# Three images of a channel norm moved into the state-space scan, and the scan's B products written in place

## What is computed

```python
x_dbl = einsum('bkdl,kcd->bkcl', xs, x_proj_weight)         # xs: 4 directions of the image
dts, Bs, Cs = split(x_dbl, [R, R + N], axis=2)              # R = 6, N = 16 states
delta = softplus(einsum('bkrl,kdr->bkdl', dts, dt_projs_weight) + dt_projs_bias)
h = exp(d_t[..., None] * A) * h + (d_t * u_t)[..., None] * B_t[:, :, None, :]   # per position
y = einsum('bkdn,bkn->bkd', h, C_t)
...                                                          # the 4 directions are added up
mean = jnp.mean(y, axis=1, keepdims=True)
var = jnp.var(y, axis=1, keepdims=True)
return (y - mean) / jnp.sqrt(var + LN_EPS) * ln_g + ln_b
```

## Time and profile before

| | us |
|---|---|
| median of 3 runs | 5211.8 (5211.26 to 5217.86) |
| the profiled execution's own time | 5209.67 |
| its span in the trace | 5207.9 |
| first scan of the selective scan starts | 2719.7 |
| last result of the scan taken | about 5125.5 |
| norm, from its first weight load to the end | 5126.1 to 5207.9 |

### The profile page before, as it was taken

One profiled execution on the slowest core, in us unless ns is written; L12 is line 12 of the kernel. 1 busy time (PEld: TensorE's weight loads), 2 busy tenths in 40 slices (PEclk: granted clock), 3 DMA queues, 4 the chain that ended last, 5 costly groups with the idle time before them and its releaser, 6 DMA issues. The chain is left out here.

```text
span 5207.9 us, 68598 instructions
## 1 busy us (share of the span) xinstructions
PE 4496.8 (86%) x15210; PEld 2101.0 (40%) x15210; DVE 4241.3 (81%) x3460; ACT 3168.8 (61%) x6678; POOL 4079.0 (78%) x1926
## 2 busy tenths in 40 slices
PE   7998797966899999994688888889898888989897
PEld 2333463632566666663452323223222332322222
DVE  4776545554189999999549999999999999999995
ACT  5885555532011111110469888888888888888886
POOL 2544555534088898989659999999999999999993
PEclk9998998988899999997789999999999999999998
DMA  2000101137777787873318788878787778888873
GB/s 55 1 1 10 51 30 44 41 105 229 150 140 149 141 149 143 150 136 60 104 44 200 199 203 201 197 201 201 202 201 191 199 200 202 202 200 202 201 202 94
DMA packets 389221, 733.15 MB, mean 141 GB/s; under 512 B 78332, under 2 KB 119464, under 8 KB 375912
## 3 DMA queue, kind: packets, MB, share of 16 engines
q1 hardware_dynamic: 388968, 730.30, 59.2%
HBM read 594.31 MB, written 82.32 MB: 130 GB/s over the span
## 5 line engine op out<-in xcount | busy, mean ns | idle before, releaser
L2221 POOL TENSOR_TENSOR l_hc<-l_h,l_c_rep 128x1024 f32<-128x1024 f32 x768 | 1797.7, 2370 | 17.9 <-DVE l_h L2292 15.6
L1400 POOL TENSOR_TENSOR l2b_prod<-l2b_v,l2b_attn 128x1568 f32<-128x1568 f32 x276 | 937.4, 3444 | 232.5 <-ACT l2b_attn L1361 117.5
L2292 DVE TENSOR_TENSOR_SCAN l_h<-l_p,l_h,l_bu 128x1024 f32<-128x1024 f32 x448 | 1027.2, 2331 | 4.8 <-ACT l_bu L2129 3.5
L1976 PE MATMUL l_p<-l_stacked,l_pick 96*128 96x512 f32 x1536 | 559.9, 446 | 220.4 <-DVE l_h L2292 203.1
L1448 DVE TENSOR_REDUCE l2b_osum<-l2b_prod 128x32 f32<-128x1568 f32 x384 | 665.7, 1780 | 63.0 <-POOL l2b_prod L1400 59.3
L2210 POOL TENSOR_TENSOR l_pool_bu<-l_du_rep,l_b_sb 128x1024 f32<-128x1024 f32 x256 | 607.6, 2373 | 37.7 <-DMA l_du_rep<-du_scratch 37.5
L2276 DVE TENSOR_TENSOR l_bu<-l_du_rep,l_p 128x1024 f32<-128x1024 f32 x512 | 612.9, 1197 | 21.5 <-DMA l_du_rep<-du_scratch 16.0
L1353 ACT ACTIVATE l2b_logits<-l2b_conv,l2b_this_b 98x512 f32<-98x512 f32 x96 | 66.1, 689 | 860.9 <-PE l2b_conv L1318 860.9
L1976 PEld LDWEIGHTS l_p<-l_stacked,l_pick 96*128 96x128 f32 x1536 | 242.3, 189 | 800.4 <-DVE l_h L2292 643.2
L1985 PE MATMUL l_p<-l_hc,l_y_pick 128*32 128x512 f32 x3072 | 523.4, 606 | 5.9 <-POOL l_hc L2221 5.6
L2292 DVE TENSOR_TENSOR_SCAN l_h<-l_p,l_h,l_pool_bu 128x1024 f32<-128x1024 f32 x224 | 524.2, 2340 | 3.8 <-ACT l_pool_bu L2129 2.8
(11 more groups left out here) (269 smaller groups left out, 8933.6 us busy)
## 6 DMA issues: line engine op xcount, KB each, us to landing
l_du_rep<-du_scratch SPq DMA_DIRECT2D x1536, 256.0 KB, 4.8
l2b_img_high<-qkv_scratch SPq DMA_DIRECT2D x192, 306.2 KB, 5.6
l2b_img_low<-qkv_scratch SPq DMA_DIRECT2D x192, 306.2 KB, 9.4
l_stacked<-l_parts SPq DMA_DIRECT2D x512, 96.0 KB, 3.2
l2b_v<-v_scratch SPq DMA_DIRECT2D x192, 152.0 KB, 6.6
qkv_scratch<-l2a_strip SPq DMA_DIRECT2D x32, 840.0 KB, 5.2
du_scratch<-l_du SPq DMA_DIRECT2D x128, 192.0 KB, 2.1
l_w_raw<-L_w_sed SPq DMA_DIRECT2D x32, 576.0 KB, 3.7
```

Of the source, the lines that this page charges most:

```text
L1400: return eng.tensor_tensor(dst.rearrange("q x (dy dx) -> q x dy dx", dx=WIN), window, attn_half[:, :, unit % 2].rearrange("q x (dy dx) -> ...
L1976: pe.matmul(p_da[p % 2][:, e, :], pick[:, GRP[i] % (Q // DL), :], stacked[:, par, GRP[i] * DL // Q, :], start=True, stop=True).then_inc(s_ ...
L2221: pool.tensor_tensor(hc[:, slot:slot + 2, :], h[:, 2 * p:2 * p + 2, :], c_rep[:, par, :].unsqueeze(1).to_broadcast([128, 2, N]), ALU.mult) ...
L2292: dve.tensor_tensor_scan(flat(h[:, 2 * p:2 * p + 2, :]), flat(p_da[p % 2]), flat(of), state, ALU.mult, ALU.add).then_inc(s_h, 1)
```

## The change

Nothing of what is computed changes. Four things move:

1. **Norm of an image in the next one's scan.** In images 1 to 3, each of the two passes of each direction's loop (c = 2, 3 and c = 4, 5) also handles one norm tile of the image before: 8 tiles an image, 24 in all, each spread over an even and an odd step. The last image's 8 tiles stay in `channel_norm_out`.
2. **Its instructions.** Even step: PE `norm_mm` (the product with `center`) ahead of `replicate(n, k, 0, par)`, into the PSUM bank of B that is free then; ACT `norm_early` (Square and Copy) between `decays 0` and `log_1e`. Odd step: PE `norm_mm` (the product with `mean_w`) at the same place; ACT Ln ahead of `log_1e` and Exp (`norm_rstd`) behind it; DVE the product `xc * rstd`, both in SBUF, between `scan 2` and `times_b 4`; ACT `norm_result` (the affine, into `X`) between `b_copy` and `decays 4`. The next `b_mm` waits for ACT to have read the bank.
3. **B products in place.** `du_rep` becomes six fixed slots of a pair; DVE and POOL write their products back into the slot and the scan reads them there. `bu` and `pool_bu` are gone, and with them the waits for a free buffer. A slot's next transfer now waits for the slot's scan instead of for a product of the ring.
4. **Loops.** Image 0 is written out ahead of the loop, the loop covers images 1 and 2, image 3 stands behind it. SP's loop body becomes a whole direction and also stores two finished tiles of `X` per direction (192 KB each). The three norm weights are loaded at the start of `selective_scan`.

```diff
+            def norm_mm(n, tile, par):
+                pe.wait_ge(s_bu, NB * n + BU0)
+                pe.wait_ge(s_bcp, n)
+                bank = p_b[1 - par][0:C]
+                if par == 0:
+                    pe.matmul(bank, center[:], X[:, bass.ds(tile * N, N)], start=True, stop=True).then_inc(s_xc, 1)
+                else:
+                    pe.wait_ge(s_xsq, tile + 1)
+                    pe.matmul(bank, mean_w[:], rstd[:], start=True, stop=True).then_inc(s_var, 1)
...
+                if tile is not None:
+                    norm_mm(n, tile, par)
                 pe.wait_ge(s_stack[par], stack_count(b, k, c, par))
                 replicate(n, k, 0, par)
...
+            def norm_early(tile, par):
+                bank = p_b[1 - par][0:C]
+                if par == 0:
+                    act.activation(rstd[:], bank, ACT.Square)
+                    act.activation(xc[:], bank, ACT.Copy).then_inc(s_xsq, 1)
+                else:
+                    act.activation(rstd[:], bank, ACT.Ln, bias=eps[:, 0:1], scale=WIDE_VAR_SCALE).then_inc(s_lnv, 1)
...
                 decays(n, k, c, 0)
+                if tile is not None:
+                    norm_early(tile, par)
                 if n1:
                     log_1e(n + 1)
+                if tile is not None and par:
+                    norm_rstd(tile)
                 decays(n, k, c, 1)
...
+                if tile is not None and par:
+                    norm_result(tile)
                 decays(n, k, c, 4)
...
                 scan(n, k, c, 2, par)
+                if tile is not None and par:
+                    dve.wait_ge(s_rstd, tile + 1)
+                    dve.tensor_tensor(xc[:], xc[:], rstd[:], ALU.mult).then_inc(s_xhat, 1)
                 times_b(n, 4, par)
...
-                dve.tensor_tensor(bu[:, at % 2], du_rep[:, slot:slot + 2, :],
+                dve.tensor_tensor(du_rep[:, p], du_rep[:, p],
                                   p_b[par].unsqueeze(1).to_broadcast([128, 2, N]), ALU.mult).then_inc(s_bu, 1)
...
-                user, step_of = (i - RING) % G // 2, (i - RING) // G
-                if user in POOL_PAIRS:
-                    sp_.wait_ge(s_pbu, NP * (n + step_of) + POOL_PAIRS.index(user) + 1 + PBU0)
-                else:
-                    sp_.wait_ge(s_bu, NB * (n + step_of) + DVE_PAIRS.index(user) + 1 + BU0)
+                if not (isinstance(n, int) and n == 0):
+                    sp_.wait_ge(s_h, PAIRS * (n - 1) + p + 1 + H0)
```

More of the change, by code:

```diff
@@ L1705, in local_attention_layout, with selective_scan @@
     }
-def selective_scan(nc, w, X, du_d):
+def selective_scan(nc, w, X, du_d, norm, out):
     K, S, R, DL = 4, 16, 6, 8
@@ L1807, in all_steps, with at, image @@
         def all_steps(step):
-            def at(b, k, c, par, last, eng=None):
+            def at(b, k, c, par, last, tile=None):
                 first = isinstance(b, int) and b == 0 and k == 0 and isinstance(c, int) and c == 0
                 step(b, b * STEPS + (k * CHUNKS) + c, k, c, par, ahead(b, k, c, 1, last), ahead(b, k, c, 2, last),
-                     None if first else ahead(b, k, c, -1, last))
-            def image(eng, b, last):
+                     None if first else ahead(b, k, c, -1, last), tile)
+            def image(eng, b, last, normed):
                 for k in range(K):
@@ L1914, in _ @@
[L1914 to L1923 removed]
+                if not (isinstance(n, int) and n == 0):
+                    sp_.wait_ge(s_h, PAIRS * (n - 1) + p + 1 + H0)
+                    sp_.nop(nofuse=True)
@@ new lines, in replicate_du, with prepare @@
+                for e in range(2):
+                    i = 2 * p + e
+                    src = du_d[par, GRP[i] * DL:(GRP[i] + 1) * DL]
+                    src = bass.AP(src.tensor, src.offset, [[0, S], [N, DL], [1, N]])
+                    sp_.dma_start(du_rep[:, p, e], src).then_inc(s_dur[p], 16)
+            def prepare(m, par):
+                store_du(m, par)
+                for p in range(SPLIT):
+                    replicate_du(m, par, p)
+                if not (isinstance(m, int) and m == 0):
+                    sp_.wait_ge(s_rep, G * (m - 1))
+                    sp_.nop(nofuse=True)
+                restack(m, par)
+                for p in range(SPLIT, PAIRS):
+                    replicate_du(m, par, p)
@@ new lines, in step, with store_tile, direction @@
+            def step(n, par, more):
+                if more:
+                    prepare(n + 1, 1 - par)
+            prepare(0, 0)
+            def store_tile(b, j):
+                tile = b * PER_IMAGE + j
+                sp_.wait_ge(s_res, tile + 1 + RES0)
+                sp_.nop(nofuse=True)
+                sp_.dma_start(out[bass.ds(b, 1), :, bass.ds(j * N, N)].rearrange("b c t -> (b c) t"),
+                              X[:, bass.ds(tile * N, N)]).then_inc(s_out, 16)
+            def direction(first, k, b, pairs):
+                for q in range(pairs):
+                    step(first + 2 * q, 1, True)
+                    step(first + 2 * q + 1, 0, True)
+                    if b is not None and q >= 2:
+                        store_tile(b - 1, 2 * k + (q - 2))
@@ L2001, in y_whole, with step @@
                 mm.then_inc(s_ysum, 1)
-            def step(b, n, k, c, par, n1, n2, before):
+            def step(b, n, k, c, par, n1, n2, before, tile):
                 if k == 0 and isinstance(c, int) and c == CHUNKS - 2:
@@ L2023, in step @@
                 if n1:
-                    b_mm(n + 1, 1 - par, *n1)
+                    b_mm(n + 1, 1 - par, *n1, tile)
                 replicate(n, k, 4, par)
@@ L2202, in times_b @@
                     pool.nop(nofuse=True)
[L2203 to L2210 removed]
+                pool.wait_ge(s_dur[p], replicated(n))
+                pool.nop(nofuse=True)
+                pool.tensor_tensor(du_rep[:, p], du_rep[:, p], b_sb[:, par, :].unsqueeze(1).to_broadcast([128, 2, N]),
                                    ALU.mult).then_inc(s_pbu, 1)
@@ L2315, in _, with channel_norm_out @@
             dve.wait_ge(s_y, B * STEPS + Y0)
-def channel_norm_out(nc, w, X, out):
+def channel_norm_out(nc, X, norm, out):
     DEPTH = 4
@@ L2494, in build @@
         attention_out(nc, w["L2"], X, o_d, x_d)
-        selective_scan(nc, w["L3"], X, du_d)
-        channel_norm_out(nc, w["L3"], X, out)
+        norm = {n: ctx.enter_context(nc.sbuf_tensor("l3n_" + n, shape, F32))
+                for n, shape in (("center", [C, C]), ("mean_w", [C, C]), ("cols", [C, 2]), ("eps", [C, 2]))}
+        selective_scan(nc, w["L3"], X, du_d, norm, out)
+        channel_norm_out(nc, X, norm, out)
 def kernel(**inputs):
```

166 lines of the change are left out of this document (76 added, 90 removed).

## The result

The changed kernel takes 5222.26 us (5217.04 to 5229.19), the kernel before, in the same rounds, 5213.58 (5207.86 to 5220.25): a ratio of 1.0015 with a 95% interval of 1.0009 to 1.0021. The prediction was 5212, with 5202 to 5222 as the forecast's own range and 5178 to 5246 as the whole: the result lies at the upper end of the first. A difference of 9 us out of 5200 hides two large ones: the norm at the end got 57 us shorter and the scan 67 us longer.

What follows compares the result with a forecast made beforehand. DVE and POOL were taken as full in the scan. Terms +55.2 - 51.1 - 2.5 + 1.0 - 2.6 = 0.0 on a span of 5207.9 gave 5212 us, own range 5202 to 5222, whole range 5178 to 5246.

Steps and rivals of the forecast that it cites:

- The bound and the mechanism: In the scan, DVE and POOL are full; decays later than DVE wants stop it, and it never makes that up.
- the working: Lateness of ACT and DVE followed through a direction's four norm steps: 4.6 us per two tiles, 55 over 12 directions.
- The product on PE, 0.7 a step: PE's norm product ahead of pair 0's replication makes ACT start pair 0 0.7 us later in each norm step.
- a product wholly hidden: Rival: PE's norm product fits in gaps, so 22 us instead of 55, 5179; chance 0.32, wholly or by half.
- ACT's terms: ACT's added norm instructions in the scan: 0.49 us each for Square, Copy and Ln, 0.5 for Exp and the affine.
- DVE's product, 14 us: 24 norm products on DVE in the scan at 0.58 us each, 14 us if nothing else were late.
- Directions that differ: Direction 0 has smaller room (ACT turns the image), directions 0 and 2 a shorter y_whole product; taken to cancel.
- Jumps: Image loop covers two images instead of three, so one jump back goes: -2.6 us, between 0 and twice that.
- The end: Norm at the end: 24 of 32 tiles go, 51.1 us, and the wait for the weights, 2.5 us.
- The three weights at the start: Their three transfers join eight others ahead of the scan: +1.0 us, between 0 and 1.8.
- The rival at POOL's port: In the scan, DVE's product of two SBUF inputs waits for POOL: 5232, or 5260 for whole instructions; chance 0.15.

Runs made afterwards that it cites:

- with the pause filled: Changed kernel with PE's product for dt done twice in the odd norm steps, ahead of pair 5's replication: 5205.4 us, ratio 0.9989.
- the product of 3539.61: From the changed kernel with ACT's Square, Copy, Ln and Exp moved into its pause ahead of pair 2: 5227.6 us, ratio 1.0028.
- the slowest kernel: Changed kernel with PE's and ACT's norm work moved and DVE's product, both inputs in SBUF, placed ahead of scan 2: 5246.4 us, ratio 1.0072.
- the two kernels whose pauses at the place shown were 0.81 and 0.79, or 0.53: Changed kernel with only DVE's product reading PSUM, ahead of scan 2: 5202.8 us; changed kernel with PE's dt product done twice: 5205.4 us.

## Why the prediction came out, and which steps of it did not

**The bound and the mechanism: right.** DVE and POOL are full, and what DVE loses it doesn't make up behind the norm steps (c = 6 and 7 are 1.4 us shorter than before in all, with the pause filled). There are 86 waits for ACT, in the direction shown ahead of scans 1 and 2 of the norm steps, in the order and about the size of the working, and none ahead of scans 3 to 5. Without the falls of the clock the working comes out well: in the kernel with the filled pause the norm steps of 12 directions cost 57.9 us, or 4.8 a direction, against 55.2 and 4.6, and the direction that was worked (1) costs 4.9.

**The term that was missing: PE's clock.** The prediction counted what each late scan does to DVE. It didn't ask what PE does while DVE is late. PE's replications wait for scans, so each delay of DVE is a pause of PE, and behind such a pause the clock fell, 14 times in 24; in the direction shown the next y products and the norm product then took nearly twice as long, and made DVE late again. It is worth 17.5 us between the two spans (5216.6 - 5199.1), of which 10.0 lie in the norm steps (67.9 - 57.9) and 7.1 in the other steps and the jumps (8.3 - 1.2), most of it in the steps c = 6. It could have been asked ahead: before, too, the clock was low in two stretches of the same window, 10 us in all.

**The product on PE, 0.7 a step: too large.** Its rival, a product wholly hidden, was priced 33 us below the forecast (55 less 22). With the clock out of the way, moving it behind the replication is worth 21 (5202.8 to 5182.0; norm steps 57.6 to 36.8). In step 1 of the direction above, ACT got its first half 3506.02 - 3504.65 = 1.37 after the norm product began, where before it was 3542.39 - 3541.51 = 0.88 after the replication began: 0.5 later, where the working had 0.7.

**ACT's terms: somewhat small.** Square and Copy have the 0.48 of spacing that was taken. Ln has 3527.97 - 3527.40 = 0.57, the affine 3539.30 - 3538.59 = 0.71 and Exp 3529.11 - 3528.49 = 0.62 instead of 0.5. All three read a bias, the affine a scale too, from a column in SBUF, which Square and Copy don't; that this is the reason was not tried. The two errors on PE and ACT lie on opposite sides.

**DVE's product, 14 us: right in length, wrong in what it costs.** 0.66 as forecast, but its removal gave 3.6 at most. A product in front of a wait only shortens that wait, and the waits for ACT did grow, by 11 us.

**Directions that differ: they did cancel, by luck.** With the pause filled directions 0 to 3 cost 5.3, 4.9, 3.1 and 5.9, a mean of 4.8 beside the 4.9 of the direction that was worked. Direction 0 was to be dearer and the short y_whole to make 0 and 2 cheaper. It is direction 3, of which nothing had been said, that makes up for most of direction 2. No run shows the reason of either.

**Jumps: right for the one that went, wrong for the one that stayed.** The term was -2.6. The step c = 1 behind image 0, where the jump went, takes 19.19 us instead of 22.56, so -3.4. The same step behind the jump between images 1 and 2, which was put at nothing, takes 27.59 instead of 24.24, so +3.3, and 25.84 with the pause filled. In the changed kernel DVE stands still for longer there, and the clock was low for 14 us:

```profile
3961.20 2.35 DVE L2348 TENSOR_TENSOR_SCAN l_h<-l_p,l_h,l_du_rep 128x1024 f32<-128x1024 f32 x1 [2.41 <-ACT l_du_rep L2169]
...
3969.22 2.35 DVE L2348 TENSOR_TENSOR_SCAN l_h<-l_p,l_h,l_du_rep 128x1024 f32<-128x1024 f32 x1 [2.92 <-ACT l_du_rep L2169]
```

Outside the norm steps the scan is 1.2 us shorter than before, and 8.3 shorter with the pause filled; behind the two jumps that is 3.4 less and 1.6 more, and the rest is spread over steps of which the prediction said nothing.

**The end: 3 us too small.** -53.6 forecast (51.1 and 2.5), -56.8 measured; 53.9 of it is from the first norm product on (79.1 to 25.2, where the prediction had about 28), the rest is ahead of it, where PE no longer waits for the weights: it starts 0.7 behind the last result of the scan instead of 3.3. The three weights at the start cost nothing that shows: the first delta_u came 1.2 earlier, not 1.0 later.

**The rival at POOL's port: didn't decide here, but did once work was moved.** The prediction's reason against it was that a late DVE finds POOL out of work. It held all 24 times: POOL was idle when the product began, and its next instruction began 0.23 or 0.24 behind it, as the second. In the direction shown it had waited 0.80 for scan 2:

```profile
3537.56 2.66 POOL L2284 TENSOR_TENSOR l_hc<-l_h,l_c_rep 128x1024 f32<-128x1024 f32 x1 [0.80 <-DVE l_h L2348]
```

It took 2.66 where the same instruction takes 2.36 elsewhere: the port cost POOL 0.3, and nothing that shows in the time (57.9 against 57.6, above). All 24 products were short. As soon as a move cured the lateness, the product met POOL at work, and the port took back what the move had won. Its price in the prediction, at most one POOL instruction (2.33), was too small: a product took 5.3 more where it met a row of them.

So 5212 against 5222 is close in part because errors cancelled. Against the span before, in us:

| | forecast | changed kernel | with the pause filled |
|---|---|---|---|
| norm steps | +55.2 | +67.9 | +57.9 |
| other steps and jumps | -2.6 | -1.2 | -8.3 |
| start | +1.0 | -1.2 | -1.0 |
| end | -53.6 | -56.8 | -57.3 |
| sum | 0.0 | +8.7 | -8.7 |

Without the falls of the clock the time would have been some 9 us below the forecast; their 17, which no term named, took it to 9 above. Each of the two is about the size of what a measurement of this kernel can tell from nothing.

## What to carry to other kernels

Read for each engine where it waits and how long, and put added work into such a pause: the same four ACT instructions cost some 31 us more ahead of the decays than in a pause of 1.19. When an engine in a ring of waits becomes late, ask what TensorE does meanwhile, and read its clock in windows as short as the pauses, for a mean of 0.98 against 0.99 hid some 15 us. Beside a full POOL give DVE products at most one SBUF input; the other can come from PSUM if its producer writes it there.

## What the runs showed of the hardware

**The wait at the port was, nearly always, for POOL to run idle.** The Trainium skill ("SBUF — State Buffer", Who interferes with whom) has the second of two contending instructions blocked until the first is done. The direction agrees, 0.66 against 6.02 us. The length does not: the product of 3539.61 waited through the POOL instruction that it met and two more that began after it, until POOL had none left. So did all seven of that kernel, and 23 of the 24 products of the slowest kernel, which ended 0.5 to 0.6 us behind the end of POOL's row. The 24th took 0.94 and got in between two POOL instructions back to back, and in the earlier trace rows a product got in after 0.98 more, with POOL still in a row of five. What makes the difference was not tried. One input from PSUM ended it, as that section says of instructions with at most one SBUF input: 24 of 24 products at 677 to 683 ns.

**The clock falls for short pauses, but not for each.** In the direction shown it fell from 2.4 to 1.2 GHz some 2 us behind a pause of PE of 1.39 us with one of 0.20 on either side (0.9 to 2.5 us behind the long one in the other 13 places), and stayed low for 3.4 us with PE busy throughout. At the jump between images it fell half a microsecond before a pause of 3.17 ended, and stayed low for 14 us. In the two kernels whose pauses at the place shown were 0.81 and 0.79, or 0.53, it did not fall there. The length of one pause doesn't decide it: 1.39 stands in all 24 odd norm steps of the changed kernel, and the clock fell behind 14 of them, never in direction 2. In the kernel without DVE's product no pause there is longer than 0.94, with 0.79 behind it, and it fell as often.

**One long wait is worse than its length.** A product of 6.02 us left PE idle for 6.76 in a row, the granted clock was 0.50 from 3546.0 to 3552.8, and the replication behind the pause took 1.22 instead of 0.73:

```profile
3549.07 1.22 PE L2014 MATMUL l_p<-l_stacked,l_pick 96*128 96x512 f32 x2 [6.76 <-DVE l_h L2348]
```

Left open: why the clock falls behind some pauses of 1.39 and not behind others, why directions 2 and 3 differ from direction 1, and by how much the port's wait and the clock share the 84 us that one operand made.
